# Expert products of a routed layer from float16 halves, rows turned three slots ahead, one Trainium2 core

## The reference

```python
def _L0_ffn_ref(x, gate_w, w1, b1, w2, b2, shared_w1, shared_b1, shared_w2, shared_b2):
    xf = x.reshape(-1, D)
    logits = xf @ gate_w
    top_logits, top_idx = jax.lax.top_k(logits, K)
    top_gates = jax.nn.softmax(top_logits, axis=-1)
    gates = jnp.sum(jax.nn.one_hot(top_idx, E, dtype=xf.dtype) * top_gates[..., None], axis=1)
    h = gelu(jnp.einsum('nd,edh->neh', xf, w1) + b1)
    out_e = jnp.einsum('neh,ehd->ned', h, w2) + b2
    routed = jnp.einsum('ne,ned->nd', gates, out_e)
    shared = gelu(xf @ shared_w1 + shared_b1) @ shared_w2 + shared_b2
    return (routed + shared).reshape(B, S, D)
```

## Time and profile before

| | us |
|---|---|
| median of three runs | 1617.25 |
| the profiled execution | 1620.32 |
| its span in the profile | 1618.6 |
| TensorE busy in it | 1574.8 (97%) |
| VectorE, ScalarE, GpSimd busy | 1149.1, 1016.6, 486.0 |

### The profile page before, as it was taken

One profiled execution on the slowest core, in us unless ns is written; L12 is line 12 of the kernel. 1 busy time (PEld: TensorE's weight loads), 2 busy tenths in 40 slices (PEclk: granted clock), 3 DMA queues, 4 the chain that ended last, 5 costly groups with the idle time before them and its releaser, 6 DMA issues.

```text
span 1618.6 us, 27705 instructions
## 1 busy us (share of the span) xinstructions
PE 1574.8 (97%) x9392; PEld 1223.9 (76%) x9392; DVE 1149.1 (71%) x2380; ACT 1016.6 (63%) x2855; POOL 486.0 (30%) x515
## 2 busy tenths in 40 slices
PE   7989979999998999999999999999999999999998
PEld 6888866666776777777777777777777777777887
DVE  6358864543997788888888887777777777898322
ACT  4354335554366987778878778777778777874100
POOL 1000222322614433433443443443443343420000
PEclk9999989999999999999999999999999999999999
DMA  8031548885664233264343363121151131110001
GB/s 306 27 99 39 215 165 265 269 264 190 216 212 158 71 115 112 81 211 156 107 137 102 105 227 106 47 78 58 46 207 62 47 117 52 47 40 7 27 33 39
DMA packets 75813, 196.62 MB, mean 121 GB/s; under 512 B 6896, under 2 KB 27376, under 8 KB 69168
## 3 DMA queue, kind: packets, MB, share of 16 engines
q1 hardware_dynamic: 70016, 176.50, 31.8%
q0 software_dynamic: 5680, 18.62, 4.0%
HBM read 147.12 MB, written 47.97 MB: 121 GB/s over the span
## 4 chain that ended last, share of the span: by engine, by line
PE 77%; DVE 7%; DMA 2%; ACT 1%; issue 1%; POOL 1%; SPq 0%; DVEq 0%; POOLq 0%; ACTq 0%
PE bank L2523 10%; PE bank L2524 10%; PE bank L99 9%; PE bank L101 8%; PE bank L100 8%; PE bank L2585 7%; PE bank L2609 6%; PE bank L2574 5%; PE bank L1423 4%; PE bank L1443 4%; PE bank L2595 3%; PE bank L1403 1%; DMA xq_scratch<-z_xs 1%; DVE x_res L1782 1%; DMA s_rows<-x_rows,t_tok 1%
## 5 line engine op out<-in xcount | busy, mean ns | idle before, releaser
L2523 PE MATMUL bank<-t_half,t_xh 128*128 128x256 f16 (+1 forms) x1024 | 309.3, 326 | 0.7 <-DVE t_hn L2842 0.7
L2524 PE MATMUL bank<-t_half,t_xh 128*128 128x256 f16 (+1 forms) x1024 | 306.0, 326 | 0.0
L2485 POOL TENSOR_SCALAR t_ve<-t_ss 128x4 f32<-128x4 f32 (+1 forms) x128 | 25.6, 200 | 566.3 <-DVE t_ss L2838 539.3
L2740 ACT ACTIVATE t_sc<-bank,t_mx 128x128 f32<-128x128 f32 x512 | 179.9, 381 | 14.3 <-DVE t_mx L2878 8.8
L2488 POOL TENSOR_TENSOR t_rs<-t_ve,t_mhalf 128x4 f32<-128x4 f32 (+1 forms) x128 | 171.5, 1340 | 10.7
L2842 DVE TENSOR_TENSOR t_hn<-bank,t_rs 128x256 f32<-128x256 f32 (+1 forms) x256 | 130.1, 549 | 58.6 <-POOL t_rs L2488 58.3
L2523 PEld LDWEIGHTS bank<-t_half,t_xh 128*128 128x128 f16 x1024 | 100.3, 98 | 66.7 <-issue 1.4
L2524 PEld LDWEIGHTS bank<-t_half,t_xh 128*128 128x128 f16 x1024 | 100.2, 98 | 66.0
L2778 ACT ACTIVATE t_y<-bank,smooth 128x128 bf16<-128x128 f32 x512 | 139.4, 403 | 2.3 <-DVE t_cq L1303 2.3
L2609 PE MATMUL bank<-t_wp,t_cq 128*128 128x512 f16 x512 | 130.8, 379 | 0.0
L2585 PE MATMUL bank<-t_hT 128*128 128x128 f32 x1024 | 126.0, 276 | 2.6 <-ACT t_hT L2767 2.3
(11 more groups left out here) (355 smaller groups left out, 3881.9 us busy)
## 6 DMA issues: line engine op xcount, KB each, us to landing
t_xh<-xq_scratch SPq DMA_DIRECT2D x64, 512.0 KB, 3.4
t_cr<-in_ctxT_dram SPq DMA_DIRECT2D x64, 256.0 KB, 2.6
t_half<-w_half SPq DMA_DIRECT2D x12, 1024.0 KB, 7.7
y_rows<-s_y SPq DMA_DIRECT2D x39, 256.0 KB, 2.6
e_w<-in_w_units_dram SPq DMA_DIRECT2D x8, 1024.0 KB, 11.9
w_rows<-in_w_qkv_dram SPq DMA_DIRECT2D x8, 1024.0 KB, 6.0
xq_scratch<-z_xs SPq DMA_DIRECT2D x16, 512.0 KB, 3.2
t_slot<-w_plain SPq DMA_DIRECT2D x4, 2048.0 KB, 9.3
```

What stands on the lines that cost most here:

```text
L2523: nc.tensor.matmul(out, rows[:, k, kind, :], w[0][:, k, a:b], start=k == 0, stop=False)
L2524: last = nc.tensor.matmul(out, rows[:, k, kind, :], w[1][:, k, a:b], start=False, stop=k == KT - 1)
L2740: last = nc.scalar.activation(sc[:, h, :], b3[4 + part][:, n, :], ACT.Exp, bias=mx[:, h:h + 1], accum_out=sm[:, h:h + 1])
```

## The change

1. The products of the eight experts. w1, w2, the rows and the hidden are each split into a high and a low float16 half, and each product becomes three float16 matmuls (`three_products`: high x high, high x low, low x high). `up` now has the weights as the stationary operand, so that the hidden comes out already turned and `turn_hidden` goes: 24 matmuls of 128 columns. `down` has 6 of 512 columns. For this the weights of each expert, and its hidden, are scaled by powers of two found from their largest values.
2. These halves are made during the retention stage. SyncE loads the eight units' raw weights into free places, VectorE takes maxima (`maxima`), TensorE sums them over partitions (`maxima_summed`), VectorE makes scales (`scales`), ScalarE and VectorE make w1's halves (`w1_high`, `w1_low`), and GpSimd, ScalarE and GpSimd w2's (`w2_scale`, `w2_high`, `w2_low`); all are stored to DRAM. `load_expert` reads the halves from there, as many bytes as before. The loads of `wo` and the first `cn` move behind them.
3. The slots. Rows have three buffers, their halves three and the turned rows four banks; the order in round s is up(s+1), turn(s+3), down(s). VectorE makes the low half of the rows and both halves of the hidden. Three more tables by slot (`route.units`) are made in `Sorting`.
4. The attention's weight units are done in pieces, one or two in each slot, behind the slot's own work on each engine; centring stays on VectorE. High and low halves of a unit are stored together, one slot later than the high half was. `LateWeights` gets a separate semaphore after its second piece (`hi_first`). `FIRST_LOW` moves to slots 33 to 36.
5. The gates and biases `gT` and `b2` are stored to DRAM before the slots' y buffers take their place and are loaded again at the end.

The core of the diff:

```diff
+        def maxima_summed(g):
+            a, b = GROUPS[g][0], GROUPS[g][-1] + 1
...
+            pe.wait_ge(self.most_in, b + g + 1)
+            for kind in range(3):
+                last = nc.tensor.matmul(self.summed(kind, a, b), self.ones_pp[:], self.u_max[:, kind, a:b], start=True,
+                                        stop=True)
+            last.then_inc(self.most_sum, 1)
...
         projected(C - 1)
         gated(C - 1, range(1))
         scored(C - 1)
+        maxima_summed(2)
         gated(C - 1, range(1, KT))
...
+        context(0)
+        context(1)
+        for e in range(3):
+            load_unit(e)
+        context(2)
+        store_w1(0)
+        store_w1(1)
+        load_unit(3)
+        load_unit(4)
+        load_unit(6)
+        store_w1(2)
+        load_unit(5)
+        context(3)
+        for e in range(3, 6):
+            store_w1(e)
+        load_unit(7)
...
+            for e in GROUPS[g]:
+                dve.wait_ge(self.w1_in[e % 4], 16 * (e // 4 + 1))
+                v.tensor_reduce(self.u_max[:, 0:2, e], self.unit_raw[e][:], op=ALU.max, axis=AX.X,
+                                apply_absolute_value=True).then_inc(self.most_in, 1)
...
         added(0)
+        maxima(0)
+        scales(0)
+        w1_low(0)
+        w1_low(1)
         low(2)
+        w1_low(2)
...
+        for e in range(4):
+            self.re.w2_scale(pool, e)
+        for e in range(4):
+            self.re.w2_low(pool, e)
+            if e:
+                self.re.w2_scale(pool, e + 3)
+        self.re.w2_scale(pool, 7)
+        for e in range(4, E):
+            self.re.w2_low(pool, e)
...
+        for i in range(3):
+            v.tensor_tensor(self.picked[:], self.same[:], env.units3[:, i].unsqueeze(1).broadcast_to([P, N, E]), ALU.mult
+                            ).then_inc(steps, n_.one())
+            dve.wait_ge(steps, n_.now)
+            v.tensor_reduce(route.units[:, i, :], self.picked[:], op=ALU.add, axis=AX.X).then_inc(route.b1_in, 1)
...
     def up(self, pe, s):
         base = self.base(s)
-        pe.wait_ge(self.xT_in, s + 1)
-        if s >= 2:
-            pe.wait_ge(self.h_in, s - 1)
-        for k in range(KT):
-            last = self.nc.tensor.matmul(self.env.bank[2 + s % 2][:, 0:HU], self.xT[s % 2][:, k, :],
-                                         self.units.experts[:, bass.ds(base + k * HU, HU)], start=k == 0, stop=k == KT - 1)
-        last.then_inc(self.up_ps, 1)
...
+        pe.wait_ge(self.lo_in, s + 1)
...
         for i in range(HT):
+            for k in range(KT):
+                w_hi, w_lo = (self.units.experts[:, bass.ds(base + half * KT * HU + k * HU + i * P, P)]
+                              for half in range(2))
+                last = three_products(self.nc, out[:, ramp(i)], w_hi, w_lo, x_hi[:, k, :], x_lo[:, k, :], k == 0,
+                                      k == KT - 1)
+        last.then_inc(self.up_ps, 1)
...
+        for s in range(-1, SLOTS_N):
+            if s + 1 < SLOTS_N:
+                self.up(pe, s + 1)
             if s + 3 < SLOTS_N:
                 self.turn(pe, s + 3)
...
             if s >= 0:
                 self.down(pe, s)
...
+            if s + 1 < SLOTS_N:
+                halves(s + 1)
+            if s + 3 < SLOTS_N:
+                x_low(s + 3)
+            if self.unit_at(s, 1) is not None:
+                ready.sums(dve, self.unit_at(s, 1))
+                ready.means(dve, self.unit_at(s, 1))
+            if self.unit_at(s, 2) is not None:
+                for part in range(2):
+                    ready.centre_heads(dve, self.unit_at(s, 2), part)
+            if self.unit_at(s, 3) is not None:
+                ready.lo_segs(dve, self.unit_at(s, 3), ready.SEGS[0:2])
+            if self.unit_at(s, 4) is not None:
+                ready.lo_segs(dve, self.unit_at(s, 4), ready.SEGS[2:4])
+                ready.lo_plain(dve, self.unit_at(s, 4))
...
+            if s % 4 == 1 and 0 < s // 4 <= ready.count:
                 ready.store_hi(sp, s // 4 - 1)
-            if s % 4 == 1 and 0 < s // 4 <= ready.count:
                 ready.store_lo(sp, s // 4 - 1)
```

More of the change, by code:

```diff
@@ L242, in centre_heads @@
[L242 to L246, removed]
-        means = hs[:, h:h + (b - a) // P].unsqueeze(2).broadcast_to([P, (b - a) // P, P])
-        self.nc.vector.tensor_tensor(heads, heads, means, ALU.subtract).then_inc(self.centred, 1)
[L250 to L255, removed]
-        for _, a, b, f in segs:
-            self.nc.scalar.activation(self.hi[:, a:b], rows[:, a:b], ACT.Copy,
-                                      scale=self.env.wfac[:, f * KT + k:f * KT + k + 1])
@@ new lines, in sync @@
+        load_unit(7)
+        sp.wait_ge(self.w1_st[3], 16)
+        sp.wait_ge(self.w1_st[0], 32)
+        sp.dma_start(self.wo_raw[:], dram["wo"]).then_inc(self.wo_in, 16)
+        sp.wait_ge(self.w1_st[1], 32)
+        sp.dma_start(self.cn[:], dram["ctx"][0:J].rearrange("b p n -> p b n")).then_inc(self.cn_in, 16)
+        sp.wait_ge(self.halves, 13)
+        for e in range(3):
+            self.load_w2(sp, e)
+        sp.wait_ge(self.p_ps, C * KT)
+        self.load_w2(sp, 3)
+        for e in range(6, E):
+            store_w1(e)
@@ L449, in scalar @@
         for c in range(C):
+            for e in W1_HI.get((c, -1), ()):
+                w1_high(e)
             for h in range(KT):
@@ L1336, in load_expert @@
     def load_expert(self, sp, u):
-        sp.dma_start(self.experts[:, u * UW:(u + 1) * UW], self.env.dram["w_units"][u]).then_inc(self.experts_in, 16)
+        for i, half in enumerate(("w1_half", "w2_half")):
+            sp.dma_start(self.experts[:, (2 * u + i) * UW:(2 * u + i + 1) * UW],
+                         self.env.dram[half][u].rearrange("p s n -> p (s n)")).then_inc(self.experts_in, 16)
     def load_shared(self, sp, ready, u):
@@ L1442, in down @@
         for i in range(HT):
-            last = self.nc.tensor.matmul(self.env.bank[6 + s % 2][:], self.hT[s % 2][:, i, :],
-                                         self.units.experts[:, bass.ds(self.bases[s] + (KT * HU + i * D), D)],
-                                         start=i == 0, stop=i == HT - 1)
+            w_hi, w_lo = (self.units.experts[:, bass.ds(self.bases[s] + (UW + half * HT * D + i * D), D)]
+                          for half in range(2))
+            last = three_products(self.nc, self.env.bank[6 + s % 2][:], self.h_hi[s % 2][:, i, :],
+                                  self.h_lo[s % 2][:, i, :], w_hi, w_lo, i == 0, i == HT - 1)
         last.then_inc(self.y_ps, 1)
     def tensor(self, pe):
-        for s in range(-3, SLOTS_N):
-            if s == -2:
-                pe.wait_ge(self.route.word_in, 1)
-                pe.wait_ge(self.units.experts_in, 16 * E)
-            if s == -1:
-                self.so.turn_gates(pe)
+        self.turn(pe, 0)
+        self.so.turn_gates(pe)
+        pe.wait_ge(self.route.word_in, 1)
+        pe.wait_ge(self.units.experts_in, 32 * E)
+        self.turn(pe, 1)
+        for s in range(-1, SLOTS_N):
+            if s + 1 < SLOTS_N:
+                self.up(pe, s + 1)
             if s + 3 < SLOTS_N:
                 self.turn(pe, s + 3)
-            if 0 <= s + 2 < SLOTS_N:
-                self.up(pe, s + 2)
-            if 0 <= s + 1 < SLOTS_N:
-                self.turn_hidden(pe, s + 1)
             if s >= 0:
```

424 lines of the change are left out of this document (286 added, 138 removed).

## The result

The changed kernel takes 1633.48 us (median of four runs, 1629.44 to 1643.02), the kernel before 1617.8 beside it: a ratio of 1.0094, 95% interval 1.0069 to 1.0119. It is slower by 11 to 19 us; the forecast was 16 us faster. The profiled execution took 1631.29 us with a span of 1628.6.

A forecast was written before the change was run, and what follows sets the result against it. TensorE was taken to bound the kernel nearly everywhere. Slots -25, preparation +5.6, cn +0.5, start +1 and end +1.5 gave -16.4 us from 1617.25, so 1601 us, range 1588 to 1618.

The forecast's parts named there:

- the cover of the grouped stores: Routed slots: ScalarE's wait for grouped high and low stores, up to 1.5 us each four slots, costed at nothing; uncovered 12 us.
- A store must land within about 6 us: Routed slots: with two buffers of y, each y store must land within about 6 us; no cost was added.
- The slot: Routed experts: 4.10 us falls to 3.45 while units move, bounds 3.1 and 3.7; 25 us gained with the last seven slots.
- the term for the transfers: Routed slots: the DMA queues' packets need 3.36 us a slot if they never rest; 3.45 taken with gaps.
- The preparation: Experts' halves, 0 to 90 us: three sums of maxima cost TensorE 5.6 us, between 1.2 and 11; cn's slip adds 0.5.
- rival 3: Preparation costs double, through SyncE's queue delaying cn or GpSimd holding the row factors: 8 us more, 1609 us; chance 0.15.
- w2 on GpSimd: 88 to 142 us: eight scalings and differences take 43 us, done at about 142, before row factors due by 149.
- Start and end of the slots: Routed stage: first up from 224.3 to about 229, first down 1 us later; 1.5 us more at the end.
- Rival 1: Routed slots: computing register addresses on TensorE's sequencer becomes the bound, 4.05 us a slot, 1624 us; chance 0.12.
- Rival 2: Routed slots: transfers give way and VectorE keeps up, 3.1 us a slot, 1590 us; chance 0.15.
- Rival 4: Routed slots: 128-column matmuls run at 0.08 us each, a slot of 3.7 us, 1607 us; chance 0.05.
- Rival 5: Halves cost what they save: VectorE, with new waits on stores, at 3.9 us a slot, 1618 us; chance 0.05.

The follow-up runs named there:

- e5: Changed kernel with the stores of a unit's high part one slot earlier, apart from the low ones: ratio 1.0008 to the kernel before.
- e1: Changed kernel with the 39 stores of y issued by ScalarE on its own queue, no longer by SyncE: 1623.51 us, ratio 1.0030 to the kernel before.
- e4: Changed kernel with three buffers of y and two of gathered rows, queues as they are: ratio 1.0053 to the kernel before.
- f3: Kernel before the change with only the high stores of a unit one slot later, together with the low ones: ratio 1.0010 to the kernel before.
- e12: Changed kernel with y stored from ScalarE's queue and the high stores a slot earlier, no other edit: ratio 0.9981 to the kernel before.
- e9: Changed kernel with y on ScalarE's queue, earlier high stores, unit 5 before 6, later third sum, w2's halves on ScalarE and VectorE, cn before w2's stores: 1609.86 us.
- e7: Changed kernel with unit 5 loaded ahead of unit 6, third sum of maxima two gate blocks later, VectorE's scales behind its scores: 1626.79 us, ratio 1.0067.
- e10: Changed kernel with e5's earlier high stores and e7's edits to the preparation, y still in SyncE's queue: ratio 0.9967 to the kernel before.
- e3: Changed kernel with the third and fourth loads of cn each ahead of one more store of w2 in SyncE's queue: ratio 1.0067 to the kernel before.
- e11: e9 with the second to fourth loads of cn issued by GpSimd's queue once their buffer is free: ratio 0.9930 to the kernel before.
- f2: e9 with 39 unused 128 KB copies between places in device memory added in SyncE's queue, one a slot: ratio 0.9979 to the kernel before.
- e6: Changed kernel with w2's halves made on ScalarE (high, with scale) and VectorE (low), nothing of it on GpSimd: ratio 1.0092 to the kernel before.
- f1: e9 with w2's halves given back to GpSimd: ratio 0.9957 to the kernel before.

## Why the prediction was wrong

**Where it failed: the cover of the grouped stores.** "Up to 1.5 us on ScalarE each four slots, covered by `down` being one slot behind. Without that cover it is 8 x 1.5 = 12 us." There was no such cover. The wait came to 16.6 us on ScalarE (up to 3.3 at a time), and taking the grouping away made the kernel 14 us shorter (e5). The price without cover was near that, and it was left out of the sum. That it came so near is partly luck, since the 14 us hold the issue of the stores in SyncE's queue too, which the step did not price. What the step missed is that SyncE issues these stores only after `y`, so whatever delays `y` delays them: once `y` was out of their way this wait was 2.9 us (e1) and 0.2 (e4), with the grouping as it was. And the slot by which it is covered had just been shortened: f3 shows the same grouping at nothing in the old slot.

**The same for `y`.** "A store must land within about 6 us" stood without a price. Before, it landed within 5.8 us and had 8.2; after, stores behind a unit's load took 7.3 to 9.2. It was the first wait that the shorter slot uncovered: 30.3 us of ScalarE's time. Taking it out of SyncE's queue gave 10 us (e1), but that took most of the other wait with it, so 14 and 10 are not the prices of two separate waits; together they are worth 18 (e12). The load and this store were neighbours in SyncE's queue in the kernel before too, but issued 2.0 to 3.7 us apart, and now 0.4. There too the store landed 0.7 to 2.3 us after the load. A sum that shortens the period has to ask this of every transfer, not only of those that the diff touches.

**The slot.** Array work of 3.04 us: 3.13 measured, right. 3.45 while units move: 4.23 in the changed kernel, but 3.55 with both edits of the stores (e12) and 3.54 in e9, where the engines' share from 300 to 350 us is 0.91 and 0.95. So the term for the transfers (3.36 if they never rest) was sound, as the floor; the forecast took the floor for the value, and 4.23 lies outside its bound of 3.7. Of the 22.5 us forecast for the slots with `hidden(0)`, 6 came by the mean of five profiles, and 0.8 in the changed kernel's own. The last slots, forecast 0.7 shorter each, were not: from the thirty-first to the thirty-ninth `y` it was 31.2 us against 30.2, with the shared units' loads ahead of `y` in the same queue.

**The preparation: +16 by the mean of five profiles, +12.6 in the changed kernel's own, forecast +6.** The first sum was forecast at 2.1 and took 2.1 (1.25 of wait, 0.80 of matmuls). The second was forecast at 0.4 and took 3.5, and 1.7 more behind it by the clock: "loads are in by about 66" failed, since unit 5 stands behind a store that took 9.2 us to land behind 3 MB of loads, and came at 68.2. The third was forecast at 3.2 and took 2.1. Even the matmuls were 0.8 each and not 0.4. `cn`, forecast at 0.5 in all, took 3.5 more of wait at the third output product (4.8 against the 1.3 that TensorE waited there before) and 2.5 by the clock. These come to 15 us, of which some 2 came back in waits that TensorE had before the sort anyway. For the sums e7 and e10 show it; for `cn` it is read from the trace, and no experiment took it away (e3, e11). That is rival 3's mechanism, to which I gave 0.15, and in size it went past it.

**w2 on GpSimd.** A scaling took 2.8 to 4.3 us (estimated 3.0) and a difference 2.1 to 2.3 (2.40): nearly right in size, the scalings some 3 us longer in all. It ended at 149.4 us and not at 142, since ScalarE's last high halves came late, and still the row factors, at 150.9, waited 1.5 us for VectorE and not for it. What I costed at nothing is below.

**Start and end of the slots.** Counted from the rows' first turn, the first `up` came 4.7 us later than before (forecast 4.7) and the first `down` 0.8 (forecast 1). From the last `y` to the first product of gates it was 12.3 us against 10.8, the 1.5 of the forecast; but ahead of that `y_out` stood 5.0 us, from 385 on, for a store behind a shared unit's load: the same mechanism once more.

**The rivals.** Rival 1 (TensorE's sequencer) did not happen, for the reason given against it. Two views of one slot of 3.13 us, lines 103 and 105 (line 104 has three more):

```profile
L103 PEldq FUSED_REGOPS  x9: 46/46/46, 249.5 to 252.2; - x9
L105 PEldq FUSED_REGOPS  x8: 46/46/46, 249.4 to 252.4; - x8
```

20 addresses, most of them 0.124 us apart, 2.5 us in all, hidden. Its side of the result, slower, came true by other means. Rival 2 (transfers give way, 3.1) did not happen: no kernel went below 3.52 a slot, and more bytes made it longer (f2). Rival 4 (0.08 a matmul) by 0.055; the Trainium skill's 81 ns ("TensorE: Matmul & The Clock Gate", "Back-to-back issue gap") doesn't hold for these pairs of load and matmul. Rival 5 named VectorE with new waits on stores as the mechanism and 3.9 us a slot as the size. The waits on stores came, but on ScalarE; with the costs of rival 3 they are what happened. I had put them apart, at 0.05 and 0.15, and never together. Two sums of the prediction also don't come out: 3.7 a slot with the preparation at 9 adds up to 1612 and not to the range's 1618, and rival 4 to 1606 and not 1607. The measured time lies outside either way.

## What to carry to other kernels

When a change shortens a period, list every transfer whose landing was hidden by the old one, with its landing time and its place in its queue, and price each at the new period; a store of `y` close behind a 1 MB load landed just after the load here. A cover that the change itself shortens is no cover: put the uncovered price into the sum. And a wait on TensorE can cost more than its length (2.65 and 4.8 us cost 1.7 and 2.5 more in slower matmuls here), so move a small step between engines to where its operands are long done, as e7 did.

## What the runs showed of the hardware

GpSimd's tensor operations stretch VectorE's. VectorE's group of normalising steps (128x512, fp32) in the kernel before from 90 to 140 us, and in the changed one from 98 to 150, when GpSimd works on w2:

```profile
L780 DVE TENSOR_SCALAR v_yn<-v_o_sb,v_mv,v_rs 128x512 f32<-128x512 f32 x12 | 5.7, 543 | 0.1
```

```profile
L945 DVE TENSOR_SCALAR v_yn<-v_o_sb,v_mv,v_rs 128x512 f32<-128x512 f32 x12 | 13.7, 1200 | 0.1
```

And four of them beside what ran on GpSimd (timeline):

```profile
117.73 4.87 DVE L945 TENSOR_SCALAR v_yn<-v_o_sb,v_mv,v_rs 128x512 f32<-128x512 f32 x4
```

```profile
118.31 2.28 POOL L407 TENSOR_TENSOR a_w_half<-a_w_raw,a_w_half 128x1024 f16<-128x1024 f32 x1
120.58 3.01 POOL L402 TENSOR_SCALAR a_w_raw<-a_w_raw,a_u_scale 128x1024 f32<-128x1024 f32 x1
```

Single steps took up to 2.4 us against 0.54, and operations on two tensors (L954) up to 2.6 against 0.69; with w2 on VectorE and ScalarE (e6) no normalising step took over 0.55 us. GpSimd's own scalings ranged from 2.8 to 4.3 us. In this stage VectorE had slack, so it cost little that can be shown (f1).

A mix of loads, stores and gathers reached 316 GB/s at a share of 0.95 (e9) and 327 at 0.96 (f2), where the kernels before and after moved 265 and 269 at 0.81.
